# Splitting two stages of matmuls into passes that fill 32 output rows each

## The reference, cut to what matters

```python
def _gn(v, G=32, eps=1e-5):              # group norm over 4 channels x 256 x 256
    g = v.reshape(B_, G, C_ // G, H_, W_)
    return ((g - mean) / sqrt(var + eps)).reshape(v.shape)

def _L0_conv_ref(x, W, b):
    u = mean(x, axis=1)                  # over the 128 channels of a pixel
    s = sqrt(var(x, axis=1, ddof=1))
    n_x = (x - u) / (s + 1e-6)
    n_x = einsum('bchw,oc->bohw', n_x, W) + b
    return x * n_x

x = x + _L0_conv_ref(_gn(x), W, b)       # x: (8, 128, 256, 256) float32
```

## Time and profile before

| | us |
|---|---|
| median of 3 runs | 2044.33 (2043.82 to 2044.66) |
| the profiled execution's own time | 2040.34 |
| its span in the trace | 2038.5 |
| PE busy (matmuls) | 1729.9, 85% |
| PEld busy (weight loads) | 738.8, 36% |
| DVE busy | 1769.1, 87% |
| ACT busy | 1371.2, 67% |
| POOL busy | 1409.6, 69% |

### The profile page before, as it was taken

The page is one execution under the profiler, slowest core; times in us unless marked ns, Lnnn a source line. Parts: engine busy times, 40 slices in busy tenths (PEclk is TensorE's granted clock), DMA queues, the critical chain, the costliest instruction groups (busy, mean ns, idle before and its releaser), DMA issues.

```text
span 2038.5 us, 39651 instructions
## 1 busy us (share of the span) xinstructions
PE 1729.9 (85%) x12322; PEld 738.8 (36%) x12322; DVE 1769.1 (87%) x1864; ACT 1371.2 (67%) x2114; POOL 1409.6 (69%) x1364
## 2 busy tenths in 40 slices
PE   0079988998799987999879998899979999899997
PEld 0024433343334333433334433334333433344443
DVE  5649989999799997999779997899979998788888
ACT  5598865887568874787748886588856887434441
POOL 0058766877577776787667876677766777688884
PEclk9979999999899999999999999999999999899999
DMA  9998998999889998999979999799988999664684
GB/s 380 357 350 313 378 356 287 418 349 401 296 312 412 327 408 286 345 382 368 376 268 383 365 383 352 279 415 349 394 324 315 416 336 405 241 228 187 246 299 198
DMA packets 188755, 687.13 MB, mean 337 GB/s; under 512 B 21200, under 2 KB 21584, under 8 KB 188496
## 3 DMA queue, kind: packets, MB, share of 16 engines
q1 hardware_dynamic: 114768, 415.63, 55.7%
q10 hardware_dynamic: 73728, 268.47, 32.9%
HBM read 415.57 MB, written 268.44 MB: 336 GB/s over the span
## 4 chain that ended last, share of the span: by engine, by line
PE 35%; DVE 18%; DMA 16%; issue 13%; POOL 12%; ACT 3%; SPq 2%; ACTq 0%; POOLq 0%; DVEq 0%
PE proj_ps L753 19%; PE sums_ps L742 10%; DMA tiles<-x 9%; DMA out<-tiles 7%; PE factor_ps L728 6%; DVE scaled L652 5%; POOL tiles L472 4%; DVE approx L683 4%; DVE tiles L665 4%; POOL tiles L461 3%; SPq L428 2%; POOL miss L479 2%; POOL pieces L491 1%; DVE bn L696 1%; DVE bn L697 1%
## 5 line engine op out<-in xcount | busy, mean ns | idle before, releaser
L753 PE MATMUL proj_ps<-scaled,w_t 128*128 128x512 f32 x2048 | 988.9, 606 | 0.2 <-DVE scaled L652 0.2
L472 POOL TENSOR_SCALAR tiles<-tiles,out_shift 128x1024 f32<-128x1024 f32 x512 | 573.9, 1121 | 281.2 <-DVE tiles L665 279.7
L544 ACT ACTIVATE squares<-tiles 128x1024 f32<-128x1024 f32 x512 | 538.2, 1051 | 314.0 <-POOL tiles L461 147.3
L461 POOL TENSOR_SCALAR tiles<-tiles,norm_scalars 128x1024 f32<-128x1024 f32 x512 | 622.1, 1216 | 144.7 <-DMA tiles<-x 132.4
L665 DVE SCALAR_TENSOR_TENSOR tiles<-proj_ps,gate_shift,tiles 128x1024 f32<-128x1024 f32 x512 | 649.0, 1268 | 72.3 <-PE proj_ps L753 69.3
L652 DVE TENSOR_TENSOR scaled<-tiles,factor_ps 128x1024 f32<-128x1024 f32 x512 | 619.0, 1209 | 47.9 <-PE factor_ps L728 35.6
L529 ACT ACTIVATE unused<-tiles,bn 128x1024 uint8<-128x1024 f32 x560 | 634.9, 1134 | 17.8 <-DMA tiles<-x 17.8
L728 PE MATMUL factor_ps<-pieces,pick_sb 128*128 128x256 bf16 x2048 | 317.9, 279 | 186.2 <-DVE scaled L652 104.9
L753 PEld LDWEIGHTS proj_ps<-scaled,w_t 128*128 128x128 f32 x2048 | 357.4, 195 | 261.2 <-issue 253.8
L742 PE MATMUL sums_ps<-tiles,const_sb 128*32 128x256 f32 x4096 | 334.4, 397 | 22.5 <-ACT squares L544 19.3
L742 PE MATMUL sums_ps<-squares,const_sb 128*32 128x256 f32 x4096 | 320.4, 384 | 0.0
(11 more groups left out here) (56 smaller groups left out, 630.0 us busy)
## 6 DMA issues: line engine op xcount, KB each, us to landing
tiles<-x SPq DMA_DIRECT2D x792, 512.0 KB, 8.9
out<-tiles ACTq DMA_DIRECT2D x512, 512.0 KB, 6.6
const_sb<-const SPq DMA_DIRECT2D x1, 193.5 KB, 2.4
scaled<-w SPq DMA_DIRECT2D x1, 64.0 KB, 2.1
scaled<-ident SPq DMA_DIRECT2D x1, 64.0 KB, 2.0
pick_sb<-pick SPq DMA_DIRECT2D x1, 8.0 KB, 2.1
bias_sb<-bias SPq DMA_DIRECT2D x1, 0.5 KB, 2.2
```

The costliest lines, as they stand in the source:

```text
L461: nc.gpsimd.tensor_scalar(place(s), place(s), norm_scalars[:, 0:1], norm_scalars[:, 1:2], ALU.add, ALU.mult).then_inc(normed, 1)
L472: nc.gpsimd.tensor_scalar(place(s), place(s), 1.0, out_shift[:, 0:1], ALU.mult, ALU.add).then_inc(finished, 1)
L544: nc.scalar.activation(squares[:, step % 2, :], place(step), ACT.Square).then_inc(squared, 1)
L753: mm = nc.tensor.matmul(proj_ps[:, s % 2, h:h + BANK], w_t[:, :], scaled[:, s % 2, h:h + BANK], start=True, stop=True)
```

## The change

In `spread` and in `project` each matmul becomes four. Matmul q takes a quarter of the stationary columns (32 of them) and writes the output rows q to q+31; the moving operand is the same for the four. Chunks, banks, waits and the instruction that increments the semaphore (now the last of the last four) stay.

```diff
                 for h in range(PARTS):
                     for t in range(TILES):
                         j = (s % SPLIT * PARTS + h) * TILES + t
-                        mm = nc.tensor.matmul(factor_ps[:, chunk(h, t)], pick_sb[:, j:j + 1].to_broadcast([P, P]),
-                                              pieces[:, s // SPLIT % 2, :], start=True, stop=True)
+                        for q in range(0, P, 32):
+                            mm = nc.tensor.matmul(factor_ps[q:q + 32, chunk(h, t)], pick_sb[:, j:j + 1].to_broadcast([P, 32]),
+                                                  pieces[:, s // SPLIT % 2, :], start=True, stop=True)
                 mm.then_inc(factors_spread, 1)
...
                 for h in range(0, SLOT, BANK):
-                    mm = nc.tensor.matmul(proj_ps[:, s % 2, h:h + BANK], w_t[:, :], scaled[:, s % 2, h:h + BANK],
-                                          start=True, stop=True)
+                    for q in range(0, P, 32):
+                        mm = nc.tensor.matmul(proj_ps[q:q + 32, s % 2, h:h + BANK], w_t[:, q:q + 32],
+                                              scaled[:, s % 2, h:h + BANK], start=True, stop=True)
                 mm.then_inc(projected, 1)
```

## The result

The changed kernel took 2029.14 us (median of 6 runs, 2019.62 to 2035.32), the kernel before 2044.49 beside it: ratio 0.9924, interval [0.9895, 0.9952]. A second set of runs gave 0.9896 [0.9873, 0.9919]. So it is 0.8 to 1.0% faster, some 15 to 21 us, where 34 had been forecast. The direction and PE's step were right; the gain was about half of the forecast.

What follows compares the result with a forecast made beforehand. The bound varied by stretch: PE with 10.9 us off it in the last period, all engines full in middle cycles. Gains of 9.4 and 24.5 made 34 us: 2006 against the profiled 2040.3, forecast 2010, range 1988 to 2050.

Steps and rivals of the forecast that it cites:

- PE's step: Steady step on PE, spread to spread: from 3.26 to 3.02 us, by closing gaps of 0.10 and 0.14 us.
- Four narrow passes cost one wide one, the spread too: On PE, four passes of 32 columns take one wide pass's time: projection stays 1.72 us, spread 0.44.
- The upper end for the spread: Spread on PE: 4 x 0.02 = 0.08 us more per step if a weight load just misses fitting beside its group.
- fed too slowly: Rival: 96 PE instructions a step arrive too slowly; at 40 ns each, 3.84 us a step and 2100 us; 12 in 100.
- the four don't run together: Rival: passes reading the same source are served one after another; step 9.6 us, time over 4900; 4 in 100.
- the gaps stay: Rival: the 0.10 and 0.14 us come from the change of stage; step stays 3.26 us, time 2044; 12 in 100.
- Middle periods, the five full cycles, at most 1.0 us each: Middle periods' 8-slot cycles: PE's part shrinks 1.2 us, DVE waits only 1.1, so at most 5 us a period.
- DMA takes some of it back: Middle periods: nearly full DMA turns cycle savings into later waits on loads; 0 to 6.5 us gained, 3.5 taken.
- Last period, 1.2 us a cycle, 9.4 in all: Last period: five PE steps on each cycle's chain gain 5 x 0.235 = 1.2 us; 8 cycles give 9.4 us.
- What would show it: Signs: step 3.02 to 3.04 us, last-period cycle 26.1, middle cycles 27.0 to 27.5, DVE's waits for PE nearly gone.
- The clock: PE's clock: narrow passes alone raised it from 1.2 to 2.4 GHz in the rows; costed at nothing.
- The range: Whole time, 1988 to 2050 us: said to hold nearly all of the forecast and the first rival, some 82 in 100.

Runs made afterwards that it cites:

- the two kernels with one stage each: Against the kernel before, only the spread in narrow passes: 2070.55 us, ratio 1.0131; only the projection in narrow passes: 2052.67 us, ratio 1.0033.
- DVE relieved: Second bn_stats of each DVE statistics slot over 32 pixels instead of 512: 2036.48 us on the kernel before, 1999.05 on the changed kernel.
- the half stores: Each store writes only the first 512 of its 1024 pixels: 2001.08 us on the kernel before, 1978.55 on the changed kernel.
- one small edit to line 675: Variance kept in PSUM, so line 675 reads PSUM instead of SBUF: 2006.91 us on the changed kernel, 2030.40 on the kernel before.

## Why the prediction was right or wrong

- *PE's step* (3.02 us, from 3.26): right, 3.02. Both gaps lay at the changes between wide and narrow; the two kernels with one stage each show it.
- *Four narrow passes cost one wide one, the spread too*: right. The upper end for the spread, 0.08 us, was not needed; its loads of 97 ns fit. The Trainium skill's statement on the fast weight load (TensorEngine Tiling (Array Packing), Tile-to-Partition Mapping, Restrictions), that column tiling switches it off, made no difference here: 97 ns for a narrow load, 99 for a wide one. No run shows whether the wide one was a fast one.
- The rivals *fed too slowly* and *the four don't run together* are refuted by the same step. 96 PE instructions went out in 3.02 us, 31 ns each.
- The rival *the gaps stay* is refuted by the loads that now go out under the passes.
- *Middle periods, the five full cycles, at most 1.0 us each*: this is the step that failed. I took 1.0 us of DVE's 1.1 us of waiting for PE as gain. The full cycles gained 0.39, 0.39 and 0.48 us. Over the five cycles that I had counted it was 1.7 us and not up to 5 (1.25 for the four in 112 us, 0.48 for the fifth). Two things were wrong. The 1.1 us come from one cycle, the first of its period; in the second DVE waited for PE for 0.50 us only and was busy for 27.67 of 28.26, and I didn't ask whether the others were like the one I read. And less waiting is not the same as gain: even in the first cycle the waits only went from 1.12 to 0.67 us, and part of that went into a longer line 675, which waits for POOL. With DVE relieved the same passes give 0.93 to 1.11. In my sum the seven middle periods stood at 24.5 us, 3.5 each; the two profiled executions gained 14.7 and 9.2 there, 2.1 and 1.3 each.
- *DMA takes some of it back*: not in the full cycles, as the half stores show. Its share of 0.99 to 1.03 was no bound there. I had used DMA to shade the estimate down, and DVE should have been the reason. Whether DMA took some of the gain in the rest of a period is not settled.
- *Last period, 1.2 us a cycle, 9.4 in all*: mis-sized, 6.0 for the period. Six cycles gained 0.91, the seventh 0.69, and the steps behind it, which have no sums, nothing; I had counted eight alike. As to the 0.91: four whole steps on the chain give 4 x 0.247 = 0.99 us, and the fifth counts only up to its projection. Behind that come DVE's gate and POOL's line 472, which starts behind the gate and which line 675 waits for, in the kernel before as well. In the two chains of waits there are 4.33 us from the fifth projection's start to DVE's `scale` before (1860.95 to 1865.28), and 4.37 after (1844.59 to 1848.96). I had followed the chain that the profile showed, through the sums, and not the one through the gate and POOL. My cycle of 27.35 us is 27.37 by its own rows (1874.65 - 1847.28), which changes nothing.
- *What would show it*: DVE's waits for PE went down (before the gate from 69.3 to 53.0 us, before the scale from 35.6 to 26.0), but were not nearly gone. POOL's waiting for loads rose from 132.4 to 136.5 us. I had expected middle cycles of 27.0 to 27.5 us and 26.1 in the last period; they were 27.37 to 27.87, and 26.45.
- *The clock*, costed at nothing: its mean was 0.975 before and 0.976 after.
- *The range* of 1988 to 2050 holds the 2029 measured, but it also held no change at all; the forecast of 2010 was 19 us off.

What stays open: how the gain of a period divides outside the full cycles. The last 19 steps of a period changed by anything from -3.5 to +1.1 us between the two profiles. In the kernel before they take from 71.4 to 78.7 us from one period to another, so nothing can be told from that. The first six steps of a period took 0.27 us longer in six of the seven.

## What to carry to other kernels

When an engine gets faster by a known amount, read its neighbour's waits for it in every repetition of the pattern and not in one. Here the smallest, 0.50 us, was near the 0.39 to 0.48 us gained, and the larger ones were not gained. A stretch in which the neighbour is busy for 98% gives little (0.39 of 28.26 us), and a DMA share of 1.0 doesn't prove that DMA binds. Count changes of matmul shape in the order on PE: converting one of the two wide stages gained nothing and lost 1.3% in one case, converting both gained 0.24 us a step. After such a gain look at what stands in front now, here DVE, and relieve that. Moving four slots of statistics brought 11 us, and only with narrow passes; one small edit to line 675 brought some 13, and the two together no more than the one. That small edit was there to take before the change too, at 12 us.

## What the runs showed of the hardware

- Passes that fill 32 output rows each and stand side by side start 3 to 4 ns apart in the changed stages and 7 in the sums, and run together, also when all four read the same moving operand (16 passes of 512 columns in 1.72 us). Four such passes cost the same as one that fills 128 rows.
- A change from passes over 128 rows to passes over 32, or back, cost 0.10 to 0.14 us at 2.4 GHz (granted clock 1.00), and 0.2 us before a float32 stage of 128 columns: the next weights were not loaded under the running pass, as they are elsewhere.
- A DVE `tensor_scalar` from SBUF to SBUF waited for the running POOL instruction to end, up to 0.9 us, and in the trace of before it ended 144 to 148 ns behind it; alone it took 293 ns. From PSUM it took 424 ns and never waited.
